# A four-layer conditional kernel: first stationary blocks in three parts, nine warm-up matmuls for fourteen

## The reference

```
x = x + L0(x)   # x W0^T + 2 * sum over the two best of 8 experts, weighted by softmax(logits + bias):
                #   (x A_e) B_e, rank 16
x = x + L1(x)   # a 64 x 64 matrix per sample, chosen out of 16, over the 64 rows of the sample
x = x + L2(x)   # (x B_a) A_a, rank 16, adapter a per sample out of 64
x = x + L3(x)   # x W3^T + b + 2 * (x A_m) B_m, rank 16, mapping m per sample out of 32
```

## Time and profile before

| | |
|---|---|
| median of 3 runs | 905.37 us (905.13 to 907.52) |
| the profiled execution | 906.27 us |
| its span | 904.5 us |
| TensorE busy | 895.8 us, 99% of the span |
| VectorE, ScalarE, GpSimd busy | 62%, 38%, 26% |
| TensorE's share of the chain that ended last | 92% |

### The profile page before, as it was taken

How to read it: one execution, slowest core, us unless ns; L and a number is a source line. 1 busy time by engine, 2 the same in 40 slices (tenths; PEclk the granted TensorE clock), 3 DMA queues, 4 the chain that set the end, 5 groups by cost and what they waited for, 6 DMA issues and landing times.

```text
span 904.5 us, 14862 instructions
## 1 busy us (share of the span) xinstructions
PE 895.8 (99%) x4758; PEld 795.4 (88%) x4758; DVE 557.5 (62%) x1421; ACT 345.8 (38%) x800; POOL 234.9 (26%) x379
## 2 busy tenths in 40 slices
PE   9999999999999999999999999999999999999997
PEld 7888888888888888998998998998998999989997
DVE  6655444354357526567667677677676676676675
ACT  5543343333334333333434433434424334334333
POOL 1000010011010003523424433424415325324240
PEclk9999999999999999999999999999999999999999
DMA  7978686999663564666766766766666567666664
GB/s 248 309 252 287 208 252 202 311 338 270 186 190 119 172 211 132 189 179 185 218 181 189 216 188 182 210 194 192 190 197 213 168 189 226 182 174 216 184 199 155
DMA packets 105602, 187.69 MB, mean 208 GB/s; under 512 B 15926, under 2 KB 66870, under 8 KB 105526
## 3 DMA queue, kind: packets, MB, share of 16 engines
q1 hardware_dynamic: 105526, 186.76, 67.7%
HBM read 143.20 MB, written 49.81 MB: 213 GB/s over the span
## 4 chain that ended last, share of the span: by engine, by line
PE 92%; DMA 3%; SPq 2%; issue 1%; POOL 1%; DVE 0%; ACT 0%; DVEq 0%; POOLq 0%
PE ps_o L1407 28%; PE ps_d L1433 17%; PE ps_w L1441 13%; PE ps_d L1441 10%; PE ps_s L1407 9%; PE ps_o L1454 5%; PE ps_d L1448 4%; PE ps_o L1465 2%; DMA mdraw<-t 2%; PE ps_s L1471 1%; SPq L445 1%; PE ps_w L1448 1%; DMA chunk_a_raw<-mov 1%; SPq L473 1%; PE ps_o L1503 1%
## 5 line engine op out<-in xcount | busy, mean ns | idle before, releaser
L1042 DVE TENSOR_TENSOR stat_lo<-stat_raw,stat_hi 128x1024 fp32r<-128x1024 f32 (+1 forms) x127 | 146.3, 1152 | 25.8 <-ACT stat_hi L773 23.5
L773 ACT ACTIVATE stat_hi<-stat_raw 128x1024 fp32r<-128x1024 f32 (+1 forms) x127 | 116.8, 933 | 20.5 <-POOL stat_raw L657 6.3
L1433 PE MATMUL ps_d<-w_hi,stat_hi 128*128 128x512 f32 x256 | 105.0, 410 | 0.0
L1433 PE MATMUL ps_d<-w_lo,stat_hi 128*128 128x512 f32 x256 | 101.1, 395 | 0.0
L1433 PE MATMUL ps_d<-w_hi,stat_lo 128*128 128x512 f32 x256 | 100.8, 394 | 0.0
L1407 PE MATMUL ps_o<-chunk_a_hi,stat_hi 128*128 128x512 f32 x216 | 84.4, 391 | 0.6 <-DVE chunk_a_lo L1042 0.6
L1407 PE MATMUL ps_o<-chunk_a_lo,stat_hi 128*128 128x512 f32 x216 | 84.1, 389 | 0.0
L1407 PE MATMUL ps_o<-chunk_a_hi,stat_lo 128*128 128x512 f32 x216 | 84.0, 389 | 0.0
L682 POOL CAST w_hi<-mdraw 128x512 fp32r<-128x512 f32 x32 | 19.6, 614 | 208.8 <-DMA mdraw<-t 208.8
L657 POOL TENSOR_TENSOR stat_raw<-stat_raw,ident 128x128 f32<-128x128 f32 x40 | 21.8, 546 | 186.3 <-DMA stat_raw<-stat 186.3
L1407 PE MATMUL ps_o<-chunk_b_hi,stat_hi 128*128 128x512 f32 x152 | 59.1, 389 | 0.0
(11 more groups left out here) (226 smaller groups left out, 2269.7 us busy)
## 6 DMA issues: line engine op xcount, KB each, us to landing
up<-tu SPq DMA_DIRECT2D x124, 256.0 KB, 4.4
stat_raw<-stat SPq DMA_DIRECT2D x59, 512.0 KB, 4.2
mdraw<-t SPq DMA_DIRECT2D x128, 208.0 KB, 2.9
stat_raw<-x SPq DMA_DIRECT2D x32, 512.0 KB, 3.5
out<-outb SPq DMA_DIRECT2D x30, 512.0 KB, 5.4
t<-md_a SPq DMA_DIRECT2D x16, 576.0 KB, 5.8
rows_raw<-x SPq DMA_DIRECT2D x32, 256.0 KB, 3.5
chunk_a_raw<-mov SPq DMA_DIRECT2D x24, 256.0 KB, 5.2
```

The lines of the kernel that those rows point to most:

```text
L773: return nc.scalar.activation(dst, src, ACT.Copy)
L1042: return nc.vector.tensor_tensor(out=dst, in0=src, in1=rounded.bitcast(F32), op=ALU.subtract)
L1433: last = nc.tensor.matmul(plain_bank(t)[:, 0:WCOLS], rows[a][:, k, :], w[c][:, k, :], start=k == 0 and m == 0, stop=k == KB - 1 and m == l ...
```

## The change

The stationary blocks of groups 0 and 1 are loaded and split in three parts of two, two and four row blocks (`PARTS`), and not in two halves. The order of loads, roundings and rests is now: part 0 of group 0, piece 0, part 0 of group 1, piece 1, part 1 of both, pieces 2 and 3, part 2 of both, pieces 4 to 7. TensorE waits for the part that holds row block k. The warm-up has 9 matmuls in place of 14. A part of two row blocks is 128x256 elements, 128 KB in 128 rows of 1 KB. (`act_half` and `dve_half` become `act_part0` and `dve_part0`; `half_hi` and `half_lo` become `part_hi` and `part_lo`.) In the changed program line 426 is line 431, 390 is 395, 773 is 781, 1042 is 1053, 657 is 665, 1402 is 1416 and 1407 is 1421.

```diff
+    PARTS = (slice(0, KB // 4), slice(KB // 4, HALF_KB), slice(HALF_KB, KB))
...
-    def halves(g, h):
+    def parts(g, h):
 
         return h * TOGETHER + g + 1
+
+    def part_of(k):
+        return [h for h, own in enumerate(PARTS) if own.start <= k < own.stop][0]
...
-        ld_half = [[sem(f"ld_half{n}_{h}") for h in range(2)] for n in range(TOGETHER)]
+        ld_part = [[sem(f"ld_part{n}_{h}") for h in range(len(PARTS))] for n in range(TOGETHER)]
...
-            load_half(0, 0)
+            def load_part(g, h):
+                own = PARTS[h]
+                sp.dma_start(sraw[g][:, own, :], stat[GROUPS[g][1]][:, own, :]).then_inc(ld_part[g][h], 16)
+
+            load_part(0, 0)
             load_piece(0, 0)
-            load_half(1, 0)
-            for k in range(1, HALF_KB):
+            load_part(1, 0)
+            load_piece(0, 1)
+            load_part(0, 1)
+            load_part(1, 1)
+            for k in range(2, HALF_KB):
                 load_piece(0, k)
-            load_half(0, 1)
-            load_half(1, 1)
+            load_part(0, 2)
+            load_part(1, 2)
             for k in range(HALF_KB, KB):
                 load_piece(0, k)
...
                     if g < TOGETHER:
-                        pool.wait_ge(ld_half[g][s // HALF_KB], 16)
+                        pool.wait_ge(ld_part[g][part_of(s)], 16)
...
+            def part_hi(g, h):
+                own = PARTS[h]
+                if h == part_of(GROUPS[g][1]):
                     act.wait_ge(pool_stat, stat_adds(g))
                 else:
-                    act.wait_ge(ld_half[g][h], 16)
-                round_to(st[g][hi][:, own, :], sraw[g][:, own, :]).then_inc(act_half, 1)
+                    act.wait_ge(ld_part[g][h], 16)
+                round_to(st[g][hi][:, own, :], sraw[g][:, own, :]).then_inc(act_part0, 1)
...
+            def part_lo(g, h):
+                own = PARTS[h]
+                dve.wait_ge(act_part0, parts(g, h))
+                rest(st[g][lo][:, own, :], sraw[g][:, own, :], st[g][hi][:, own, :]).then_inc(dve_part0, 1)
...
-            WARM_UP = 14
+            WARM_UP = 9
...
             for k in range(KB):
                 pe.wait_ge(dve_mov, k + 1)
                 for g in range(TOGETHER):
-                    pe.wait_ge(dve_half, halves(g, k // HALF_KB))
+                    pe.wait_ge(dve_part0, parts(g, part_of(k)))
                     last = product(g, k)
```

More of the change, by code:

```diff
@@ L337, in build @@
             sem, ("pool_const", "pool_stat", "pool_mov", "pool_md", "pool_mb", "pool_mix", "pool_s", "pool_ud", "pool_udb"))
-        act_half, act_stat, act_mov, act_u3, act_ev, act_hl, act_t = map(
-            sem, ("act_half", "act_stat", "act_mov", "act_u3", "act_ev", "act_hl", "act_t"))
+        act_part0, act_stat, act_mov, act_u3, act_ev, act_hl, act_t = map(
+            sem, ("act_part0", "act_stat", "act_mov", "act_u3", "act_ev", "act_hl", "act_t"))
         act_x0, act_x1, act_s, act_part, act_ud, act_mix, act_exp = map(
@@ L343, in build @@
         act_yp, act_La, act_Lb, act_Ra, act_Rb = map(sem, ("act_yp", "act_La", "act_Lb", "act_Ra", "act_Rb"))
-        dve_half, dve_stat, dve_mov, dve_u3, dve_ev, dve_hl, dve_set, dve_t1, dve_t4a, dve_t4, dve_t = map(
-            sem, ("dve_half", "dve_stat", "dve_mov", "dve_u3", "dve_ev", "dve_hl", "dve_set", "dve_t1", "dve_t4a", "dve_t4",
+        dve_part0, dve_stat, dve_mov, dve_u3, dve_ev, dve_hl, dve_set, dve_t1, dve_t4a, dve_t4, dve_t = map(
+            sem, ("dve_part0", "dve_stat", "dve_mov", "dve_u3", "dve_ev", "dve_hl", "dve_set", "dve_t1", "dve_t4a", "dve_t4",
                   "dve_t"))
@@ L422, in store_own @@
                              source[first:first + OWN].rearrange("a p k r -> a p (k r)")).then_inc(st_own, 16)
-            def load_half(g, h):
-                own = slice(h * HALF_KB, (h + 1) * HALF_KB)
-                sp.dma_start(sraw[g][:, own, :], stat[GROUPS[g][1]][:, own, :]).then_inc(ld_half[g][h], 16)
-            load_half(0, 0)
+            def load_part(g, h):
+                own = PARTS[h]
+                sp.dma_start(sraw[g][:, own, :], stat[GROUPS[g][1]][:, own, :]).then_inc(ld_part[g][h], 16)
+            load_part(0, 0)
             load_piece(0, 0)
-            load_half(1, 0)
-            for k in range(1, HALF_KB):
+            load_part(1, 0)
[3 more added lines that the diff above has]
+            for k in range(2, HALF_KB):
                 load_piece(0, k)
-            load_half(0, 1)
-            load_half(1, 1)
+            load_part(0, 2)
+            load_part(1, 2)
             for k in range(HALF_KB, KB):
@@ L826, in t_hi @@
                 last.then_inc(act_t, 1)
-            def half_hi(g, h):
-                own = slice(h * HALF_KB, (h + 1) * HALF_KB)
-                if h == GROUPS[g][1] // HALF_KB:
+            def part_hi(g, h):
+                own = PARTS[h]
+                if h == part_of(GROUPS[g][1]):
                     act.wait_ge(pool_stat, stat_adds(g))
                 else:
-                    act.wait_ge(ld_half[g][h], 16)
-                round_to(st[g][hi][:, own, :], sraw[g][:, own, :]).then_inc(act_half, 1)
-            half_hi(0, 0)
+                    act.wait_ge(ld_part[g][h], 16)
+                round_to(st[g][hi][:, own, :], sraw[g][:, own, :]).then_inc(act_part0, 1)
+            part_hi(0, 0)
             piece_hi(0, 0)
-            half_hi(1, 0)
-            for k in range(1, HALF_KB):
+            part_hi(1, 0)
+            piece_hi(0, 1)
+            part_hi(0, 1)
+            part_hi(1, 1)
+            for k in range(2, HALF_KB):
                 piece_hi(0, k)
-            half_hi(0, 1)
-            half_hi(1, 1)
+            part_hi(0, 2)
+            part_hi(1, 2)
             for k in range(HALF_KB, KB):
@@ L1102, in t_lo @@
                 last.then_inc(dve_t, 1)
[L1104 to L1109, removed]
-            piece_lo(0, 0)
-            half_lo(1, 0)
-            for k in range(1, HALF_KB):
+            def part_lo(g, h):
+                own = PARTS[h]
+                dve.wait_ge(act_part0, parts(g, h))
+                rest(st[g][lo][:, own, :], sraw[g][:, own, :], st[g][hi][:, own, :]).then_inc(dve_part0, 1)
+            part_lo(0, 0)
+            piece_lo(0, 0)
+            part_lo(1, 0)
+            piece_lo(0, 1)
+            part_lo(0, 1)
+            part_lo(1, 1)
+            for k in range(2, HALF_KB):
                 piece_lo(0, k)
-            half_lo(0, 1)
-            half_lo(1, 1)
+            part_lo(0, 2)
+            part_lo(1, 2)
             for k in range(HALF_KB, KB):
```

## The result

The changed kernel takes 908.03 us (median of 14 runs, 905.29 to 914.03) and the kernel before, beside it, 905.27 us (14 runs, 903.95 to 907.89). The ratio is 1.0026, 95% interval 1.0014 to 1.0039. The forecast was 905.5 us with a range up to 907.0 us: by the ratio the change lost 2.4 us, near the 0.3% bound, and the median lies outside the range. The slowest run is 8.7 us above the fastest, where that of the kernel before is 3.9 us above.

The account below looks back on a forecast made before the run. TensorE, busy 99%, was taken as the bound, so only group 2's start counted. Warm-ups 0, piece 1 0 and queue +0.1 us, from 905.37 us, gave 905.5 us; range 904.1 to 907.0 us.

Parts of the forecast that it names:

- Warm-ups: TensorE's start: the stream ends at 5.40 us instead of 7.56 us, 2.15 us less before piece 0; 0 at group 2.
- The clock: TensorE at piece 0: lower level until about 7 us, some 0.43 us a matmul, piece 0 ending near 7.5 us.
- Piece 1: Head loads: 768 KB instead of 1,024 KB ahead, TensorE has it at 8.0 us, 1.6 us earlier; 0 at group 2.
- Pieces 2 and 3: TensorE's head: starts piece 2 at 10.2 us, 0.75 us earlier, and piece 3 at 11.6 us.
- The wait before piece 4: TensorE waits for VectorE's chain until 13.75 us; some 0.75 us of the gain becomes a new wait.
- The added operations: ScalarE and VectorE before 11.1 us: some 0.5 us more on each, absorbed by idle time, so 0.
- The queue: SP's loads: two more issues, last parts issued at 4.5 us instead of 3.56 us; +0.1 us on landing.
- 1 (last parts later): Group 0's last part lands after 10.06 us and delays VectorE's chain: up to 0.93 us, 906.3 us; 15%.
- 2 (the order helps): Load queue from 4 to 8 us: last parts land earlier, -1.75 us at most, likelier -0.9 us, 904.5 us; 15%.
- 3 (clock stays low): A hole between pieces 0 and 1 restarts TensorE's clock climb: group 2 at 20.2 us, +0.8 us, 906.2 us; 7%.
- 4 (loads cost as loads, 910.8 us): SP's queue: each added load keeps its own 2.7 us turn, last parts land 5.4 us later; 3%.
- 5: Head loads: the edit does nothing to piece 1, landing at 8.15 us as now; forecast's time, shares its 60%.

Follow-up runs that it names:

- g15: Kernel before, 14 warm-ups kept, plus 20 idle TensorE instructions (already fulfilled semaphore waits) just ahead of group 19: 907.03 us, ratio 1.0033 to the kernel before.
- g13: Changed kernel plus 20 idle TensorE instructions just ahead of group 19, none behind the warm-ups: 904.45 us, ratio 1.0001 to the kernel before.
- e5: Changed kernel plus 20 idle TensorE instructions behind its nine warm-ups: 904.58 us, ratio 0.9992 to the kernel before.
- g16: e5 run again unchanged: 904.65 us, ratio 0.9998 to the kernel before.
- f11: e5 plus 5 more idle TensorE instructions ahead of each of groups 4 to 7: 912.17 us, ratio 1.0072 to the kernel before.
- e2: Changed kernel with 14 warm-ups again, its three parts kept: 905.7 us, ratio 0.9998 to the kernel before.
- e8: Changed kernel with 14 warm-ups and 8 idle TensorE instructions ahead of each of groups 4 to 19: 908.52 us, ratio 1.0035 to the kernel before.
- e6: Changed kernel with 14 warm-ups and 40 idle TensorE instructions behind them: 909.36 us, ratio 1.0046 to the kernel before.

## Why the prediction was wrong

**The step that failed** is the first paragraph's: "So a microsecond gained or lost before group 2 starts has nothing later that swallows it, and the whole effect is how far the start of group 2 moves." Group 2 moved by 0.1 us in the two profiles, and by +0.2 us in the means of all traces, and the time by 2.4 us (0.26% of 905.3 us). The warm-ups were priced by their time alone, 2.15 us less in front of piece 0, and their 20 instructions were not counted as a part of the stream that has to be fetched. g15 puts a price on a shift of the same size the other way: 0.33%, 3.0 us; by g13 and the pair of e5 and g16 its undoing gives the change's whole loss back. The rows that should have warned stood there: 1.8 us of waits for `h3stack` and `h2T` after 24 us mean that the second stage has places at which a load a little late stops TensorE. I read them as small, where they are places of no slack. My own sign that the reasoning is wrong, "if TensorE's later waits change", was met: three waits for `h3stack` and one for `h2T` became two and two, at other places.

**The head, point by point.**
- *Warm-ups:* right. 18 records, first product at 5.45 us (forecast 5.4 us).
- *The clock:* right in sign, off in size. The first steps are 0.60 and 0.27 us, all from 6.3 us on 0.23 us, so the upper level was there before 6.3 us and not at 7.0 us, and piece 0 ended by 7.24 us, not near 7.5 us. The 0.43 us for the lower level was not what its working gives (twice 0.23 us is 0.46 us), but it is what f11 shows at a granted clock of 0.50. The warm-ups' weight loads still read 331 ns, as in the earlier trace rows. The Trainium skill, TensorE: Matmul & The Clock Gate (Part 1: The HAM clock gate), spoke against cutting warm-ups; at the head no run shows a price for it, since the products carried the clock up themselves.
- *Piece 1:* 7.24 us, not 8.0 us. Its split began at 6.08 us and was done at 6.77 us; the 768 KB were in over a microsecond earlier than the 6.6 us taken from the landing of group 1's first half in the earlier trace rows.
- *Pieces 2 and 3:* piece 2 at 9.32 us (10.2 us). As piece 2's split (8.58 us) no longer queues behind piece 1's, it starts 0.9 us earlier than I had it. Piece 3 follows at 10.82 us (11.6 us).
- *The wait before piece 4:* 1.20 us and not 0.7 us, at 13.54 us and not 13.75 us. Right as a mechanism; the gain ahead of it was bigger, so the wait is too.
- *The added operations:* right. The idle time of VectorE ahead of the last parts is 1.01 us as before (1.02 us).
- *The queue:* I took +0.1 us; in this pair of traces it was -0.2 us at VectorE's chain (11.59 against 11.80 us), but one pair does not decide it. Over all traces the chain starts at 11.43 to 11.82 us with halves (five, mean 11.64 us) and at 11.43 to 12.52 us with three parts (fifteen, mean 11.87 us): +0.2 us, hardly clear of the spread. In the three other profiled executions of the changed kernel group 2 starts at 19.38, 19.66 and 19.86 us; the mean of the four, 19.56 us, lies in the forecast 19.4 to 19.6 us.

**The rivals.** 1 (last parts later): in the mean of the traces a quarter of its price, not in the profiled pair. 2 (the order helps): in that pair alone, and a quarter of its price. 3 (clock stays low): no, the 0.54 us wait before piece 2 leaves the step behind it at 0.23 us. 4 (loads cost as loads, 910.8 us): no; e2 has the two added loads and 14 warm-ups and stands at 0.9998, so more and smaller loads had no price in this place. 5: no. None of the five had the mechanism.

**The numbers.** I gave 0.95 to less than 0.3% of change; the ratio's interval, 1.0014 to 1.0039, lies on both sides of that bound, and the median at 908.03 us is outside the range. All cases of the range were about the head, which came in nearly as said; a case for "the second stage is disturbed by something not read" was missing, and the kernel's own spread from 905.1 to 907.5 us in three runs was the sign that something not fixed by the program costs microseconds.

## What to carry to other kernels

In a kernel whose TensorE is busy 99% of the time and has a few waits with no slack, count the instructions that an edit adds or removes on that engine, not only their time: they move later loads of its code. Before an edit worth less than half a per cent is judged, run it once with idle instructions that restore the old stream length; if the ratio changes, what was measured was the alignment and not the edit. If the two differ, a handful of idle instructions ahead of the sensitive stage is a knob of its own: here the original length was the best of those tried, and the change with it restored (0.9992 to 1.0001) is no slower than the kernel before, but not faster either.

## What the runs showed of the hardware

- Loads of TensorE's code are DMA traffic of 16 KB a packet, 38 or 39 in a run. The median over all traces is 1.0 us and 94% take up to 1.35 us; the longest takes 2.9 us (e8).
- In 20 traces all eight `mdraw` loads over 6 us, where the median is 2.9 us, have such a load of code inside them, and none of the 2,407 without one takes over 5.2 us.
- A stream shifted by 20 of TensorE's instructions, with nothing else changed, costs 0.33% [0.16, 0.50] and widens the runs from 3.5 us (902.71 to 906.18, 35 runs) to 8.8 us (905.09 to 913.91, 12 runs).
- A wait of 2.35 us in the middle of a busy TensorE was followed by 3 us at a granted clock of 0.50, the lower of the two levels (f11). One of 2.44 us in e6 was not: there the clock reads 1.00 throughout. After the wait of 1.99 us in e8 it reads 0.57 from 733 to 736 us. In the kernel before no such stretch is there.
- Two loads more in a full queue cost 0.95 us at the point of issue. At VectorE's chain behind the landing it is -0.2 us in one pair of traces and +0.2 us in the mean of five and fifteen.
